# Moving q's product ahead of the transpositions in an attention loop, and reordering the loads and the constants of its opening

## The chip, the cores and the metric

The kernel runs on one core of a Trainium2 chip. The metric is the device time of one execution in microseconds (us); the time of a kernel is the median of its runs. The engines are TensorE (PE; its weight loads are listed as PEld), VectorE (DVE), ScalarE (ACT), GpSimd (POOL) and SyncE (SP), which here only issues DMAs. Each engine runs its instructions in the order of its own program and waits on semaphores for the others.

## What is computed

x is 8 x 256 x 128 (B batches, N rows, C columns). Attention has 16 heads of 64 with one key and value shared by all heads, a learned null key and value (the two rows of `cond_64`), a relative position bias that a small MLP produces, and a causal mask. A feed-forward part with simulated int8 quantisation follows.

```python
xn = ln(x, g_norm)
q = (xn @ Wq).reshape(b, n, 16, 64).transpose(0, 2, 1, 3)
kv = xn @ Wkv                              # k, v: one head
k, v = concat([null_k, k]), concat([null_v, v])
q = l2norm(q) * q_scale;  k = l2norm(k) * k_scale
sim = einsum('bhid,bjd->bhij', q, k) * 8 + bias   # bias from the MLP
attn = softmax(where(causal | ~mask, neg, sim))
y = ln(einsum('bhij,bjd->bhid', attn, v).reshape(b, n, 1024) @ Wout, g_out)
out = x + ffn_int8(y)                      # scales are maxima over all of y
```

## The kernel before

Everything stays on the core. The work of attention is cut into 32 groups: a batch b has four groups g = 0 to 3 of four heads each. `over_groups` (L103) runs a function `group(s)` for the first 30 of them on each engine; `Group` (L59) says which pieces of other batches and groups ride along. The last two groups, `ending`, are written out.

In group s, TensorE (L1010) makes: the values (L887, probabilities times v, into `val_ps`) of the group two before, `s.summed`; the scores of s in two pairs of heads (L865, banks `front` and `back`); the output products of `s.summed` (L843); the transpositions of the probabilities of the group before, `s.turned` (L931), two heads in the front banks, then the transposition of a quarter of q (L754), then two heads in the back banks; and at the end q's product (L740) for the quarter `s.made`, three passes in the fp32r form that together stand for fp32. Small products of the next batch's k, v and x ride in the transpositions (`low_make`, L909). A quarter of q is 128 rows times 8 heads.

A quarter of q then passes all engines: TensorE's product into the one bank `q_ps`; ScalarE squares it (`q_square`, L532) as the first thing of the next group; VectorE sums the squares per head (`q_norm2`, L1143), also first; GpSimd raises to the power -0.5 (`q_power`, L411) ahead of its probabilities; VectorE scales (`q_normalise`, L1147) between the two score pairs; TensorE transposes; VectorE copies (`qT_evac`, L1154). ScalarE's group (L611) is: square of q, exponentials of two heads of the group before, of two heads of s, then the four copies `pT_evac` (L593) that the values wait for. VectorE's group (L1323) is: q sums, copy of the values' bank (`oT_copy`, L1262), scores of the first pair (L1270), reciprocals, k and q scaling, scores of the second pair, reciprocals, `qT_evac`, and the statistics of x, k and y. GpSimd (L451) does the powers of k, y, x and q, then multiplies probabilities by the reciprocal row sums (`normalise`, L443), four instructions for a pair of heads.

The order on every engine is written out by hand. The opening prepares batch 0: SP (L337 to 348) loads x, the k/v weights, the q weights, the mask, the second layer's constants `b1b` and `g1b`, and more; ACT's queue (L495 to 502) loads the first layer's constants, w1, the key constants `condk`, `qs`, `ks` (semaphore `ld_keys`) and the null value. The MLP runs beside the first k, v and q: TensorE L776 to 807, VectorE L1175 to 1260, ScalarE L549 to 581, GpSimd L384 to 441. Its result, `table`, goes to DRAM and comes back as the bias of all rows (SP, L351 to 359). `q_ps0` (L267) names the four banks of the first batch's quarters; they are made by `q_make_first` (L749) in fp32, two passes each. `keep_busy` (L771) issues transpositions of the identity whose result nobody reads. `mask_min` (L1191) decides between the two variants of TensorE's program; `value_load` (L794) reads it.

## Time and profile before

| | |
|---|---|
| median of 3 runs | 299.69 us (299.69 to 299.98) |
| the profiled execution | 299.08 us |
| its span, first to last instruction | 297.3 us |
| granted clock of TensorE, mean | 0.970 |
| busy: PE, DVE, ACT, POOL | 257.9, 238.1, 230.0, 204.6 us |
| opening, up to the first scores of TensorE | 26.9 us |
| groups 0 to 3 | to about 60.8 us |
| six batches alike | 60.8 to 232.9 us |
| last groups, feed-forward part | to 297.3 us |

The profile is of one execution. Its times are in microseconds from the start of the span. A timeline row has the start, the duration, the engine, the line, the operation, what it writes and reads, and, in brackets, how long the engine stood idle before it and what released it. Rows with x3 or x8 are several instructions merged: the duration runs from the start of the first to the end of the last. Matmuls are pipelined, so the distance between two starts says more of TensorE than a duration. The granted clock (PEclk) is a share of 2.4 GHz.

### The profile page before, as it was taken

How to read it: one execution, taken by the hardware profiler on the slowest of the kernel's cores; microseconds unless marked ns; L12 is line 12 of the kernel's file. 1: busy time of each engine (PE TensorE's matmuls, PEld its weight loads, DVE VectorE, ACT ScalarE, POOL GpSimd, SP SyncE). 2: the span in 40 equal slices, each digit the busy share in tenths (PEclk: the TensorE clock that was granted, in tenths of full speed). 3: DMA queues.
4: the chain of work that ended last, by engine and by line, in shares of the span. 5: the costliest groups of instructions: out<-in, count | busy, mean ns of one | idle time of the engine just before them, and what ended most of it. 6: DMA issues, size and time to landing. Idle time of an engine off the chain costs nothing.

```text
span 297.3 us, 7308 instructions
## 1 busy us (share of the span) xinstructions
PE 257.9 (87%) x2161; PEld 203.5 (68%) x2162; DVE 238.1 (80%) x969; ACT 230.0 (77%) x781; POOL 204.6 (69%) x394
## 2 busy tenths in 40 slices
PE   0769999999999999999999999999999989975270
PEld 0427777787888778877887888788878767751060
DVE  2768978798879878888888798787877788869893
ACT  1554978888898899889988988889888897259380
POOL 2277979788878887887888888788877785013300
PEclk9989999999999999999999999999999999999857
DMA  4179100000000000000000000000000020000013
GB/s 142 33 191 264 21 1 2 1 2 1 3 0 2 4 1 2 0 3 1 2 0 4 3 0 2 0 4 0 2 0 4 1 73 3 2 0 0 1 37 110
DMA packets 13084, 6.89 MB, mean 23 GB/s; under 512 B 1954, under 2 KB 12914, under 8 KB 13043
## 3 DMA queue, kind: packets, MB, share of 16 engines
q1 hardware_dynamic: 11874, 6.03, 7.7%
q10 hardware_dynamic: 1168, 0.36, 0.6%
q8 instruction: 20, 0.33, 0.5%
q14 instruction: 22, 0.17, 0.2%
HBM read 5.31 MB, written 1.07 MB: 21 GB/s over the span
## 4 chain that ended last, share of the span: by engine, by line
PE 60%; DVE 20%; POOL 8%; issue 5%; DMA 4%; ACT 2%; SPq 1%; POOLq 0%; DVEq 0%; ACTq 0%
PE bank L904 14%; PE front L881 7%; PE bank L855 7%; PE back L947 7%; PE bank L744 6%; POOL prob L448 6%; PE back L881 5%; PE front L947 4%; DVE score L1276 4%; DMA g1b<-in_L_cond_g_dram 4%; PE bank L760 3%; DVE oT L1266 2%; DVE hmax L1428 2%; DVE oT L1464 2%; DVE yn L1299 1%
## 5 line engine op out<-in xcount | busy, mean ns | idle before, releaser
L589 ACT ACTIVATE prob<-score,negmax 128x258 f32<-128x258 f32 (+1 forms) x256 | 113.4, 449 | 17.8 <-DVE negmax L1276 17.7
L448 POOL TENSOR_SCALAR prob<-prob,rrow 128x258 f32<-128x258 f32 x254 | 107.9, 443 | 22.0 <-DVE rrow L1284 20.1
L401 POOL TENSOR_TENSOR rq<-qn,neghalf 128x8 f32<-128x8 f32 x32 | 53.3, 1666 | 2.7
L589 ACT ACTIVATION_READ_ACCUMULATOR prob<-score,negmax 128x1 f32 x256 | 49.2, 192 | 0.0
L904 PE MATMUL bank<-pT,val 128*64 128x256 f32 x496 | 47.1, 332 | 0.0
L1276 DVE CUSTOM_DVE_ANT_0 score<-front,bias 128x258 f32<-128x258 f32 (+1 forms) x128 | 38.2, 354 | 8.0 <-PE front L881 7.8
L904 PEld LDWEIGHTS bank<-pT,val 128*64 128x64 f32 x496 | 30.8, 136 | 19.3 <-ACT pT L599 9.9
L1145 DVE TENSOR_REDUCE qn<-sq 128x8 f32<-128x512 f32 x32 | 21.9, 684 | 23.7 <-ACT sq L535 23.7
L1276 DVE CUSTOM_DVE_ANT_0 score<-back,bias 128x258 f32<-128x258 f32 (+1 forms) x128 | 38.0, 353 | 0.1
L855 PE MATMUL bank<-wout,oT 128*128 128x128 f32 x256 | 36.7, 287 | 1.2 <-DVE yn L1299 1.1
L599 ACT COPY pT<-back 128x384 f32<-128x384 f32 x62 | 28.8, 481 | 9.0 <-PE back L947 8.6
L855 PEld LDWEIGHTS bank<-wout,oT 128*128 128x128 f32 x256 | 31.0, 191 | 5.5 <-DVE oT L1266 1.5
L947 PE MATMUL back<-ident,prob 128*128 128x128 f32 x192 | 30.4, 277 | 2.9 <-POOL prob L448 2.1
L881 PE MATMUL front<-kT,qT 64*128 64x258 f32 (+1 forms) x256 | 29.7, 350 | 0.3 <-DVE qT L1156 0.2
L947 PE MATMUL front<-ident,prob 128*128 128x128 f32 x192 | 29.6, 273 | 0.0
L599 ACT COPY pT<-front 128x384 f32<-128x384 f32 x62 | 26.9, 470 | 3.2 <-PE front L947 3.1
L881 PEld LDWEIGHTS front<-kT,qT 64*128 64x128 f32 x256 | 22.2, 186 | 7.5 <-issue 5.9
L881 PE MATMUL back<-kT,qT 64*128 64x258 f32 (+1 forms) x256 | 26.7, 327 | 0.0
L947 PEld LDWEIGHTS back<-ident,prob 128*128 128x128 f32 x192 | 21.2, 141 | 7.0 <-DVE negmax L1276 5.2
L1266 DVE COPY oT<-bank 128x512 f32<-128x512 f32 x32 | 22.1, 689 | 4.8 <-PE bank L904 2.2
L881 PEld LDWEIGHTS back<-kT,qT 64*128 64x128 f32 x256 | 22.3, 187 | 1.8 <-issue 0.3
L947 PEld LDWEIGHTS front<-ident,prob 128*128 128x128 f32 x192 | 22.8, 141 | 0.2 <-DVE negmax L1276 0.2
(203 smaller groups left out, 465.0 us busy)
## 6 DMA issues: line engine op xcount, KB each, us to landing
bias<-relative_table SPq DMA_DIRECT2D x8, 256.0 KB, 5.0
out_dram<-prob SPq DMA_DIRECT2D x4, 256.0 KB, 3.0
X<-in_x_dram SPq DMA_DIRECT2D x1, 896.0 KB, 13.9
prob<-in_L_cond_Wq_dram SPq DMA_DIRECT2D x1, 512.0 KB, 5.4
wout<-in_L_cond_Wout_dram SPq DMA_DIRECT2D x1, 512.0 KB, 15.1
prob<-in_L_ffn_w_down_dram SPq DMA_DIRECT2D x1, 176.0 KB, 2.4
X<-in_x_dram SPq DMA_DIRECT2D x1, 128.0 KB, 4.3
prob<-in_L_ffn_w_gate_dram SPq DMA_DIRECT2D x1, 128.0 KB, 2.2
```

Of the source, the lines that this page charges most:

```text
L401: pool.tensor_tensor(dst, src, neghalf[:, 0:width], ALU.pow).then_inc(done, 1)
L448: pool.tensor_scalar(prob[:, par, h, cols], prob[:, par, h, cols], rrow[:, par, h, t:t + 1], 1.0, ALU.mult, ALU.mult).then_inc(normed, 1)
L589: act.activation(prob[:, par, h, cols], score[:, h % 4, cols], ACT.Exp, scale=-1.0, bias=negmax[:, par, h, t:t + 1], accum_out=rowsum[:, p ...
L599: act.copy(pT[:, h % 4, :], bank[i][:, 0:3 * P]).then_inc(pT_ready, 1)
L744: last = pe.matmul(ps[:, :], xx[par][:, P * (q % 2):P * (q % 2) + P], ww[:, 512 * (q // 2):512 * (q // 2) + 512], start=xx is xTh and ww i ...
L855: pe.matmul(y_out(t), oT[:, m % 2, k, t * P:t * P + P], wout[:, k, :], start=k + t == 0, stop=False, skip_group_check=True)
L881: product = pe.matmul(banks[a][:, at:at + KEYS1 - c0], qT[par][rows, h // 2, t * P:t * P + P], kT[par][rows, c0:KEYS1], start=not masked, ...
L904: last = pe.matmul(ps[a * D:a * D + D, pair * N + i0:pair * N + N], val[m % 2][:, blk, :], turned[:, 2 * pair + a, c0:c1], start=blk == 1, ...
L947: product = pe.transpose(bank[i][:, k * P:k * P + P], prob[:, par, h, c0:c0 + P], ident[:, :])
L1145: dve.tensor_reduce(qn2[:, q, :], sq[:, :, :], AX.X, ALU.add).then_inc(q_n2, 1)
L1266: dve.tensor_copy(oT[:, m % 2, 2 * g:2 * g + 2, :].rearrange("p k n -> p (k n)"), (q_ps if at == GB * B - 1 else val_ps)[:, :])\
L1276: dve.tensor_tensor_reduce(score[:, h % 4, c0:c0 + w], ps[:, c0:c0 + w], bias[:, h, 0:w], -1.0, -3.0 * NEG, ALU.add, ALU.min, negmax[:, pa ...
```

## The change

Loads: `b1b` and `g1b` go ahead of the q weights and the mask on SP. GpSimd's four memsets of constants go ahead of its first power. In the opening ScalarE's mask row goes to the end, the second silu behind the squares of q's quarters 0 and 1; TensorE makes three quarters of q at once, and `keep_busy` calls are added. VectorE's `mask_min` and `table` go back in its order, and q's third scaling goes into group 0. In the loop q's product goes ahead of the transpositions, its square ahead of the pT copies, its sum ahead of `qT_evac`, its power behind the back heads' probabilities, and its scaling to the start of the next group. The values wait for their copies pair by pair. y's power goes from group 2 to group 1. The diff, cut to its core:

```diff
-        q_ps0 = [bank[i] for i in (5, 2, 3, 4)]
+        q_ps0 = [bank[i] for i in (5, 2, 4, 5)]
@@ sync
+            for dst, src in ((b1b[:, :], row(b1)), (g1b[:, :], row(g1))):
+                sp.dma_start(dst, src).then_inc(ld_mlp, 16)
             sp.dma_start(wq[:, :], Wq).then_inc(ld_wq, 16)
             sp.dma_start(mask_u[:, :], mask.rearrange("(a b) n -> a (b n)", a=1)).then_inc(ld_mask, 16)
-            for dst, src in ((b1b[:, :], row(b1)), (g1b[:, :], row(g1))):
-                sp.dma_start(dst, src).then_inc(ld_mlp, 16)
@@ gpsimd
             pool.memset(table[:, 0:P - 1], NEG).then_inc(table_pad, 1)
+            pool.memset(mrow[:, :, 0:KEYS1 + 1:P + 1], 0.0).then_inc(consts, 1)
+            pool.memset(vnull[:, :, :], 0.0).then_inc(consts, 1)
+            pool.memset(unull[:, :, :], 0.0).then_inc(null_zero, 1)
+            pool.memset(pnT[:, :], 0.0).then_inc(null_zero, 1)
...
             mlp_power(0)
-            pool.memset(mrow[:, :, 0:KEYS1 + 1:P + 1], 0.0).then_inc(consts, 1)
-            pool.memset(vnull[:, :, :], 0.0).then_inc(consts, 1)
-            pool.memset(unull[:, :, :], 0.0).then_inc(null_zero, 1)
-            pool.memset(pnT[:, :], 0.0).then_inc(null_zero, 1)
             mlp_power(1)
@@
             def group(s):
-                if s.kT is not None:
-                    k_power(s.kT)
-                if s.g == 2 and s.prev is not None:
-                    y_power(s.prev)
-                if s.g == 3 and s.b + 3 < B:
-                    x_power(s.b + 3)
-                if s.quarter is not None and s.quarter >= 4:
-                    q_power(s.quarter, s.quarter % 4)
                 if s.turned is not None:
                     normalise(heads(s.turned)[2:4])
                 if s.at == 2:
                     x_power(2)
+                if s.g == 3 and s.b + 3 < B:
+                    x_power(s.b + 3)
+                if s.g == 1 and s.prev is not None:
+                    y_power(s.prev)
+                if s.made is not None:
+                    q_power(s.made, s.made % 4)
+                if s.kv is not None:
+                    k_power(s.kv)
                 normalise(heads(s.at)[0:2])
@@ ending of gpsimd
-                y_power(B - 2)
@@ scalar, opening
             mlp_turned(0)
+            kv_evac(0, halves(misc))
+            q_square(0, q_ps0[0])
+            q_square(1, q_ps0[1])
+            mlp_silu(1)
+            mlp_turned(1)
+            q_square(2, q_ps0[2])
+            act.wait_ge(kT_done, 1)
+            for par in range(2):
+                act.copy(kT[par][:, 0:KEYS1:P + 1], misc[:, 2 * P:2 * P + 2]).then_inc(null_a, 1)
+            kT_evac(0, halves(misc))
+            v_copy(0)
+            act.activation(table_load[:, 1:2], neghalf[:, 0:1], ACT.Exp)
+            q_square(3, q_ps0[3])
+            act.wait_ge(wq_ready, 1)
+            act.copy(wqh[:, :], wq[:, :]).then_inc(wq_high, 1)
             act.wait_ge(ld_mask, 16)
...
             act.activation(keys1, mask_v, ACT.Copy, scale=-NEG, bias=NEG).then_inc(mask_ready, 1)
-            kv_evac(0, halves(misc))
-            q_square(0, q_ps0[0])
-            mlp_silu(1)
-            mlp_turned(1)
-            q_square(1, q_ps0[1])
-            act.activation(table_load[:, 1:2], neghalf[:, 0:1], ACT.Exp)
...
-            kT_evac(0, halves(misc))
-            v_copy(0)
-            for q in range(2):
-                q_square(q + 2, q_ps0[q + 2])
-            act.wait_ge(wq_ready, 1)
-            act.copy(wqh[:, :], wq[:, :]).then_inc(wq_high, 1)
@@ scalar, loop
             def group(s):
-                if s.quarter is not None and s.quarter >= 4:
-                    q_square(s.quarter, q_ps)
                 if s.turned is not None:
                     exponent(heads(s.turned)[2])
                     exponent(heads(s.turned)[3])
...
                 exponent(heads(s.at)[1])
+                if s.made is not None:
+                    q_square(s.made, q_ps)
                 if s.turned is not None:
                     pT_evac(s.turned, 0)
@@ tensor, opening
             def q_make_first(q):
+                if q == 3:
+                    pe.wait_ge(q_norm, 1)
...
                 last.then_inc(mlp_t, 1)
+                keep_busy(3, qT_ps)
                 pe.wait_ge(mlp_a, 2 * layer + 2)
...
             pe.wait_ge(consts, 3)
+            keep_busy(40, qT_ps)
             for t in range(2):
                 xT_make(0, t, halves(misc))
...
             q_make_first(1)
+            q_make_first(2)
             mlp_turn(1)
...
-            pe.wait_ge(min_ready, 1)
-            least = pe.value_load(mask_min[:, :])
...
-            q_make_first(2)
+            keep_busy(6, qT_ps)
             qT_make(0)
             q_make_first(3)
             pe.wait_ge(null_a, 2)
             pe.wait_ge(kT_ready, 1)
+            keep_busy(6, misc)
+            pe.wait_ge(min_ready, 1)
+            least = pe.value_load(mask_min[:, :])
             keep_busy(6, misc)
@@ tensor, scores
                 if s.at == 0 and pair == 1:
-                    pe.wait_ge(q_norm, 3)
+                    pe.wait_ge(q_norm, 2)
@@ tensor, values
-                if at == LOOP:
-                    pe.wait_ge(pTe_ready, GH)
-                else:
-                    pe.wait_ge(pT_ready, GH * (at if at > LOOP else at + 1))
...
                 for pair in range(2):
+                    if at == LOOP:
+                        pe.wait_ge(pTe_ready, 2 * pair + 2)
+                    else:
+                        pe.wait_ge(pT_ready, GH * (at - 1 if at > LOOP else at) + 2 * pair + 2)
@@ tensor, loop
                 if s.g == 1 and s.prev is not None:
                     y_null(s.prev)
+                if s.made is not None:
+                    if s.made % 4 == 0:
+                        if s.first:
+                            pe.wait_ge(wq_low, 1)
+                        pe.wait_ge(xT_low, s.next)
+                    q_make(s.made, s.made % 4, s.made // 4 % 2, q_ps)
                 if s.turned is not None:
                     turn(s, 0)
                     turn(s, 1)
...
                     turn(s, 3)
-                if s.made is not None:
...
-                    q_make(s.made, s.made % 4, s.made // 4 % 2, q_ps)
@@ vector, opening
-            dve.tensor_reduce(mask_min[:, :], mask_u[:, :].bitcast(U16), AX.X, ALU.min).then_inc(min_ready, 1)
...
+            k_norm2(0)
             dve.wait_ge(ld_keys, 16 * 3)
             dve.tensor_tensor_reduce(ksq[:, 2, :], condk[:, :], condk[:, :], 1.0, 0.0, ALU.mult, ALU.add,
                                      kn2[:, 2:3]).then_inc(null_v, 1)
-            k_norm2(0)
...
             q_norm2(0, 0)
-            dve.wait_ge(mlp_t, 4)
-            dve.wait_ge(ld_w2, 16 * 2)
-            dve.tensor_scalar(table[:, P - 1:TABW], bank[1][0:H, 0:N], b2c[:, 0:1], None, ALU.add).then_inc(mlp_v, 1)
+            q_norm2(1, 1)
             dve.wait_ge(qks_ready, 1)
             dve.wait_ge(k_rk, 1)
             k_scale_out(condk[:, :], 2)
             k_normalise(0)
-            q_norm2(1, 1)
+            dve.wait_ge(mlp_t, 4)
+            dve.wait_ge(ld_w2, 16 * 2)
+            dve.tensor_scalar(table[:, P - 1:TABW], bank[1][0:H, 0:N], b2c[:, 0:1], None, ALU.add).then_inc(mlp_v, 1)
             q_normalise(0, 0, q_ps0[0])
+            dve.tensor_reduce(mask_min[:, :], mask_u[:, :].bitcast(U16), AX.X, ALU.min).then_inc(min_ready, 1)
...
             q_norm2(3, 3)
-            q_normalise(2, 2, q_ps0[2])
             x_normalise(1)
@@ vector, loop
             def group(s):
-                if s.quarter >= 4:
-                    q_norm2(s.quarter, s.quarter % 4)
-                if s.summed is not None:
-                    oT_copy(s.summed)
                 if s.g == 2 and s.prev is not None:
                     y_normalise(s.prev)
+                    oT_copy(s.summed)
+                if s.quarter >= 4:
+                    q_normalise(s.quarter, s.quarter % 4, q_ps)
+                if s.summed is not None and not (s.g == 2 and s.prev is not None):
+                    oT_copy(s.summed)
+                if s.at == 1:
+                    xT_split_low(1, 1)
...
-                if s.quarter >= 4:
-                    q_normalise(s.quarter, s.quarter % 4, q_ps)
+                if s.at == 0:
+                    q_normalise(2, 2, q_ps0[2])
                 score_pair(heads(s.at)[2:4])
...
                 invert(heads(s.at)[0:2])
+                if s.g == 1 and s.prev is not None:
+                    y_stats(s.prev)
+                if s.made is not None:
+                    q_norm2(s.made, s.made % 4)
                 if s.quarter > 2:
                     qT_evac(s.quarter, s.quarter % 4, s.quarter // 4 % 2)
                 if s.at == 1:
-                    xT_split_low(1, 1)
                     x_stats(2)
```

In `ending` VectorE's `y_normalise(B - 2)` goes ahead of `oT_copy(LOOP - 2)`.

## Rows read from the trace of the kernel before

**Rows 1.** Busy us (x instructions) by engine in one batch, granted clock, DMA share, GB/s.
```profile
118.16:146.85 28.69, 28.28 (x253) 23.23 (x255) 24.54 (x109) 25.31 (x91) 24.01 (x48) 1.00 0.01 2
```
**Rows 2.** Waits from 60.77 to 232.95: us in total, times, longest us.
```profile
PEld back L947 <- DVE negmax L1276: 4.9, 12, 0.5
```
**Rows 3.** Timeline of TensorE in one group (start, duration).
```profile
154.09 1.52 PE L904 MATMUL bank<-pT,val 128*64 128x256 f32 x16
155.54 0.93 PE L881 MATMUL front<-kT,qT 64*128 64x258 f32 x8
...
159.41 0.51 PE L947 MATMUL back<-ident,prob 128*128 128x128 f32 x3
...
160.49 0.48 PE L744 MATMUL bank<-wqh,xTh 128*128 128x512 f32 x1
...
161.36 0.87 PE L904 MATMUL bank<-pT,val 128*64 128x256 f32 x8
```
**Rows 4.** Timeline of ScalarE at the end of that group.
```profile
160.77 0.48 ACT L599 COPY pT<-back 128x384 f32<-128x384 f32 x1 [0.33 <-PE back L947]
...
161.67 0.63 ACT L535 ACTIVATE sq<-bank 128x512 f32<-128x512 f32 x1
```
**Rows 5.** Timeline of VectorE: sum of q's squares, oT copy, q's scaling.
```profile
133.63 0.69 DVE L1145 TENSOR_REDUCE qn<-sq 128x8 f32<-128x512 f32 x1 [0.67 <-ACT sq L535]
134.23 0.68 DVE L1266 COPY oT<-bank 128x512 f32<-128x512 f32 x1
...
136.55 0.69 DVE L1151 TENSOR_TENSOR qn<-bank,rq 128x512 f32<-128x512 f32 x1
```
**Rows 6.** Timeline of GpSimd: q's clamp and power, four scalings of probabilities.
```profile
134.52 0.25 POOL L399 TENSOR_SCALAR qn<-qn 128x8 f32<-128x8 f32 x1 [0.33 <-DVE qn L1145]
134.85 1.67 POOL L401 TENSOR_TENSOR rq<-qn,neghalf 128x8 f32<-128x8 f32 x1
136.72 1.66 POOL L448 TENSOR_SCALAR prob<-prob,rrow 128x258 f32<-128x258 f32 x4 [0.21 <-DVE rrow L1284]
```
**Rows 7.** Chain of work that ended last, in the opening: start, us, what.
```profile
3.43 10.45 DMA g1b<-in_L_cond_g_dram
```
**Rows 8.** Timeline of all engines in the opening.
```profile
3.88 0.45 ACTq L499 DMA_DIRECT2D ks<-in_L_cond_k_scale_dram  x1
...
9.02 0.66 PE L713 MATMUL bank<-ident,xn 128*128 128x128 f32 x2 [9.02 <-DVE xn L1117]
...
10.29 1.19 DVE L1191 TENSOR_REDUCE mask_min<-mask_u 1x1 int32<-1x1024 uint16 x1
...
12.79 1.92 PE L751 MATMUL bank<-prob 128*128 128x512 f32 x2
...
13.97 0.42 DVE L1202 TENSOR_TENSOR prob<-front,b1b 128x256 f32<-128x256 f32 x1 [1.70 <-DMA g1b<-in_L_cond_g_dram]
...
16.52 0.69 ACT L542 ACTIVATE prob<-prob,mrs 128x128 f32<-128x128 f32 x2 [1.18 <-POOL mrs L401]
...
20.87 1.92 PE L751 MATMUL back<-prob 128*128 128x512 f32 x2
```
**Rows 9.** Timeline of VectorE's first scores and three idle stretches of TensorE.
```profile
28.39 0.42 DVE L1276 CUSTOM_DVE_ANT_0 score<-front,bias 128x258 f32<-128x258 f32 x1
...
36.90 0.48 PE L744 MATMUL bank<-wqh,xTh 128*128 128x512 f32 x1 [0.54 <-issue]
...
42.74 0.30 PE L727 MATMUL front<-ident,kz 128*128 128x128 f32 x1 [0.64 <-DVE kz L1134]
...
50.95 0.66 PE L760 MATMUL bank<-ident,qn 128*128 128x128 f32 x4 [0.39 <-DVE qn L1151]
```
**Rows 10.** DMA issues: count, KB, us from issue to landing.
```profile
b1b<-in_L_cond_b_dram SPq DMA_DIRECT2D x1, 64.0 KB, 6.3
...
ks<-in_L_cond_k_scale_dram ACTq DMA_DIRECT2D x1, 32.0 KB, 11.4
```
**Rows 11.** Busy us by engine and granted clock from 22 to 23, columns as in rows 1.
```profile
22.00:23.00 1.00, 1.00 (x3) 0.42 (x2) 0.00 (x0) 0.18 (x1) 1.00 (x2) 0.50 0.56 144
```

More of the change, by code:

```diff
@@ L761, in qT_make, with keep_busy @@
                 last.then_inc(qT_done, 1)
+            def keep_busy(count, ps):
+                for _ in range(count):
+                    pe.transpose(ps[:, 0:P], ident[:, :], ident[:, :])
             def mlp_turn(layer):
@@ L1356, in group @@
                     x_normalise(s.b + 2)
-                if s.g == 1 and s.prev is not None:
-                    y_stats(s.prev)
                 if s.g == 2 and s.b > 1:
```

14 lines of the change are left out of this document (2 added, 12 removed).

## The prediction

> **What bounds the kernel now.** I read the busy time by stretch first, then the waits of the loop, then one group of the loop engine by engine, and last the opening. The loop's batches take 28.69 us each and are alike; in one, TensorE's matmuls are busy 28.28 us, VectorE 24.54, ScalarE 25.31 and GpSimd 24.01 [rows 1]. So TensorE's own queue sets the pace and the others have 3 to 5 us a batch to spare. Only TensorE's small stalls can be won in the loop, plus what the opening wastes.
>
> Where are these stalls? VectorE's long waits, those for ScalarE's square of q, are off the path, since TensorE stays busy through them. What counts in the view of waits are the rows of TensorE: the back transpositions wait for VectorE's scores, 12 times in six batches, 4.9 us [rows 2]. In the group that starts at 154.09 the six back transpositions start at 159.41 and the next product at 160.49: 1.08 us for what unstalled costs 6 x 0.11 = 0.66, so 0.42 idle [rows 3]. In two of a batch's four groups this happens (here 0.42; about 0.2 in the milder one, an estimate from 4.9/12 = 0.41 of weight-load wait, half of which overlaps running matmuls). The second place: three q passes take 160.49 to 161.36 = 0.87 [rows 3], though their columns need only about 0.24 each (0.72, and some 0.07 for the change of form: 0.79). The missing 0.08 is the wait for the last pT copy: it starts at 160.77 and takes 0.48 [rows 4], so it ends at 161.25 and the values start 0.11 later. Four of those are 0.33 a batch. Idle in a batch is thus 0.42 + 0.2 + 0.33 = 0.95 to 1.0 us; in six batches 6 us. More than that the loop can't give.
>
> **The loop, part by part.** No work is added or removed; q's product, its square, its reduction, its power and its scaling each move.
>
> TensorE: three q passes (0.79) go from behind the back transpositions to ahead of the front ones. Every transposition starts 0.79 later against scores and probabilities, so the 0.42 and 0.2 vanish: both were smaller. What is late next: between the last back transposition and the values stood q as a filler of 0.87. Now nothing does. The path is last transposition's issue end, 0.28 to the copy's start, 0.48 copy, 0.11 to TensorE: 0.87 [rows 3, 4]. The split wait covers most of it: the first pair of values (half of 154.09 to 155.54, 0.73) [rows 3] needs only two copies. The remainder is 0.87 - 0.73 = 0.14 a group, 0.56 a batch, in place of 0.33. Net: 0.62 + 0.33 - 0.56 = 0.4 a batch, 2.4 us in six batches. Bounds: if queueing behind another copy adds 0.07, 0.28 a batch less, so 0.7 in all; if the remainder is hidden, 5.7.
>
> ScalarE: the square (0.63, [rows 4]) moves ahead of the four pT copies. It waits for q, which now ends some 5.1 us into a group, about when I step the exponentials to end (4.8), so it costs the copies 0.6; they are needed only from 6.9 on for the first pair. Hidden by 0.2.
>
> VectorE and GpSimd form the new risk. Now VectorE scales q by rq before its oT copy, and rq comes from GpSimd. The chain from one group to the next: y products 1.0, q 0.79, 0.2 to ScalarE, square 0.6, 0.07, reduction 0.69 [rows 5], 0.1, GpSimd's clamp and power 2.0 (134.52 to 134.85 + 1.67) [rows 6], 0.07, scaling 0.69 (0.62 until the next starts) and oT copy 0.68 [rows 5], 0.1 to the next y products: 6.8 to 6.9 us. A group takes 28.69/4 = 7.17 now and would take 7.07. So VectorE's waiting instruction holds oT copy and scores behind it, but ends some 0.2 us before TensorE asks. This is the narrowest cover of the change. Where GpSimd is busy when the reduction is done (the four probabilities, 1.66 [rows 6], start only when VectorE has inverted; a power of x or y, 0.97 at most, comes first), the chain gets longer by that overlap. I work out about 0.25 us of overlap in groups with a power of x; it eats 0.2 us, no more, and I leave it inside the bound.
>
> GpSimd otherwise gains: the probabilities of the back heads no longer stand behind a q power of 2.0 us.
>
> **The first groups.** Three idle stretches of TensorE stand here: 0.54 before the product of group 1, 0.64 before the turned k of group 2, 0.39 before q's transposition in group 3 [rows 9]. The first goes, since the low part of x is split earlier and q is asked for when VectorE is past it; the second is filled by the 0.79 of q, now ahead of it; the third came from rq standing behind two powers, and rq is now made half a group earlier. Sum 1.57, less 4 x 0.02: 1.5 us. Bounds 0.5 (only one of them) and 2.2.
>
> **The opening.** The chain now runs through g1b's landing: issued at 3.43, 10.45 us [rows 7], and VectorE's add waits 1.70 for it until 13.97 [rows 8]. Moved ahead of the q weights it should land near 8. Then the add waits for the product with w1, which I put at 11.6 to 12.4: the 1.19 us minimum of the mask [rows 8] is gone from ahead of it, but the q weights land later by b1b and g1b (0.35 + 0.45 of issue at least), and VectorE's scaling of them with it. That frees 1.6 us. But two things take it back. VectorE waits for the three key constants; ks lands 11.4 us after its issue at 3.88, at 15.3 [rows 8, 10]. And ScalarE's order has the second q square ahead of the second silu; that square waits for VectorE's first reduction, which is behind ks: 15.3 + 0.35 + 0.65 = 16.3. So silu 2 starts at 16.3 + 0.55 = 16.9 where it is 16.52 now [rows 8]. The table for the bias is then 0.3 us later, not earlier, and costs nothing as long as its loads land before the first scores (I expect 25.4 against 25.8).
>
> What gains is behind it. k's scaling follows at 17.6; three quarters of q are ready; TensorE is at full clock. From rows: the first q pieces took 0.86 a pass at 12.79 (two passes in bank 5, 1.92 with the drain), and the pieces made at 20.87 ran likewise, with a granted clock of 0.50 (1.2 GHz) in 22 to 23 [rows 8, 11]. The added transpositions (40, then 3, 3, 6, 6) use idle time; 40 cost 0.22 each at 1.2 GHz and 0.11 at 2.4, so from 1.5 us they end between 7.8 and 10.4. x is turned at 9.02 now [rows 8], so their bound is 0 to 1.4 us late; I take 0, since the clock rises on the way. The mask's minimum, 1.19, now stands between q's first scaling and the rest on VectorE, the path: it is paid there. ScalarE's mask row and the w_q split (some 3 us) end about 0.5 us before the first exponential. Stepping VectorE's queue: q scaled 20.2, minimum 21.4, reduction 22.0, qT 22.6, scaling 23.2, x statistics 23.9, qT 24.6, reduction 25.2, xn 25.8. The first scores, at 28.39 now [rows 9], come at 25.85; q's third scaling, moved into group 0, gives back 0.4. Gain 2.2 us; bounds 0 (silu, the power and ks all late) and 4.
>
> One rule speaks against the load order. Of g1b the row says that b1b, issued 0.39 us before it, landed after 6.3 us and g1b after 10.4 [rows 10]: landing is far from the order of issue. The Trainium skill, page "DMA: Bandwidth & Descriptors", section "Queues, rings and completion order", says that each engine takes turns between its queue rows and that completion isn't first in, first out; the trace agrees. By it g1b could still land near 13.9. As a mechanism of this kernel: ScalarE's queue has its own eight loads under way in that stretch. The add then stays at 13.97, the first reduction comes at 17.0 and silu 2 at 17.6: 0.7 us less than my sum, inside the bound.
>
> **Sum.** 2.4 + 1.5 + 2.2 = 6.1 us. The profiled execution took 299.08 (span 297.3 and 1.8 around it): 293.0. The median of the runs is 299.69, 0.6 above it: 293.6.
>
> **The rivals.**
> Loop gives nothing: the 0.14 at the values is 0.24, or the chain of 6.9 takes what was won. Sum 1.5 + 2.2: 296.0. For it: the cover is 0.2 us. Against: 3 to 5 us of slack an engine. 0.13.
> Opening gives nothing: ks and the ScalarE order hold all of it: 295.8. 0.08.
> It gives all: opening 4, first groups 2, loop 4.5: 289.2. 0.12.
> Neither does what it says, the waits only change place: 299.7, 0.05.
> **Slower:** the chain through GpSimd becomes the bound. Its place is VectorE's scaling of q ahead of oT copy; it decides from the point where the power begins over 0.3 us later than I have it (6.85 + 0.3 is a group of now). At 0.6 late a group is 7.45, 0.28 more, x 24 = 6.7 us; less 3.7 of the opening and first groups, about 302 to 303. For it: a 1.66 us block and a power of 0.97 share that queue. Against: VectorE inverts at 3.7 us into a group, the block ends at 5.6, the reduction at 6.3. 0.12.
>
> **How the numbers follow.** The forecast has 0.50, its own range 291.5 to 296. Range for 8 in 10: from 289.0 to 298.5, which leaves out the slower case 0.12, the case of no change 0.05 and the tail of the best one 0.03. Faster by over 0.2% (under 299.1; about what a measurement of this kernel can tell) is 0.50 + 0.13 + 0.08 + 0.12 = 0.83; same 0.05; slower 0.12.
>
> **What would show it.** Batches of 28.3 us; no wait of back transpositions on scores; a wait of 0.1 to 0.2 us in the middle of the values on ScalarE's copy; VectorE's wait for the square smaller and a new one for GpSimd's rq; first scores near 25.9; g1b landing under 9. I am wrong if oT copies end later than 3.1 us into a group, if y products wait for them, or if x is turned after 9.6.

## The result, and the profile after

The changed kernel takes 301.75 us (median; 300.96 to 303.23) where the kernel before takes 299.69: a ratio of 1.0083, 95% interval 1.0047 to 1.0119. It is slower, by 0.8%; 293.6 us, 6.1 less than before, was forecast. The profiled execution took 303.23 us, with a span of 301.4 and a mean granted clock of 0.969.

**Where the 4.1 us of span came from**, profiled execution against profiled execution. Up to VectorE's first scores: 28.63 against 28.39 [rows 9], +0.24. From there to the start of the values of group 4: 31.90 against 32.31, -0.41. Six batches, from the values of group 4 to those of group 28: 175.72 against 172.18, +3.54. The rest +0.73. So nearly all of it is in the loop, where 2.4 us of gain were forecast. (The first two are of one execution each: five kernels with after's opening, unchanged, have their first scores at 27.38 to 28.76, three with the old one at 27.97 to 28.39. A difference of a few tenths there says nothing.)

A batch of after, in the columns of [rows 1]:

```profile
119.62:149.14 29.52, 28.18 (x254) 23.48 (x255) 24.44 (x109) 24.78 (x92) 23.70 (x47) 1.00 0.01 2
```

TensorE is busy 28.18 us, 0.1 less than before, but the batch takes 29.52 where it took 28.69. By this view its idle time has grown from 0.41 to 1.34 us a batch. No engine is busy over 96% of the batch: the bound is no engine's work any more. It is a ring of waits: a chain of instructions on several engines that comes back to where it began, so that each turn can start only when the last one is through. The chain of the work that ended last says it too, by engine (before: PE 60%, DVE 20%, POOL 8%):

```profile
DVE 29%; PE 26%; POOL 18%; issue 12%; ACT 8%; DMA 4%; SPq 1%; POOLq 0%; DVEq 0%; ACTq 0%
```

Waits from 60 to 235 in after (us in total, times, longest):

```profile
DVE qn L1157 <- POOL rq L405: 24.2, 24, 1.9
ACT prob L588 <- DVE negmax L1281: 23.9, 24, 1.4
...
PEld bank L860 <- DVE oT L1271: 7.6, 12, 0.9
PE bank L860 <- DVE oT L1271: 5.2, 11, 0.7
...
PEld back L952 <- issue: 3.0, 6, 0.5
PE back L952 <- POOL prob L448: 1.8, 6, 0.3
...
ACT sq L534 <- PE bank L743: 1.5, 6, 0.3
...
PEld back L952 <- DVE negmax L1281: 0.3, 1, 0.3
```

The last row carries the name of what the change was to remove: 12 waits of the back transpositions, 4.9 us, put down to scores [rows 2]. One is left under that name. But six more, one a batch, are still there under "issue", 0.5 each, and TensorE's own row says what they wait for, before and after: GpSimd's probabilities.

```profile
160.21 0.52 PE L947 MATMUL back<-ident,prob 128*128 128x128 f32 x3 [0.29 <-POOL prob L448]
```

```profile
133.61 0.52 PE L952 MATMUL back<-ident,prob 128*128 128x128 f32 x3 [0.29 <-POOL prob L448]
```

The first rows are what came new. In each of 24 groups VectorE's scaling of q waits for GpSimd's power, 1.0 us on average. In three groups of four (all but g = 2, where it goes ahead) the oT copy that TensorE's output products (L860) need stands behind it in VectorE's queue, and in all four the next scores do. One group in detail, all from after. VectorE:

```profile
136.69 0.68 DVE L1271 COPY oT<-bank 128x512 f32<-128x512 f32 x1
137.29 0.41 DVE L1281 CUSTOM_DVE_ANT_0 score<-front,bias 128x258 f32<-128x258 f32 x1
...
140.13 0.69 DVE L1151 TENSOR_REDUCE qn<-sq 128x8 f32<-128x512 f32 x1 [0.30 <-ACT sq L534]
...
143.63 0.69 DVE L1157 TENSOR_TENSOR qn<-bank,rq 128x512 f32<-128x512 f32 x1 [1.89 <-POOL rq L405]
144.24 0.68 DVE L1271 COPY oT<-bank 128x512 f32<-128x512 f32 x1
144.84 0.42 DVE L1281 CUSTOM_DVE_ANT_0 score<-front,bias 128x258 f32<-128x258 f32 x1
```

ScalarE, first of the exponentials and the square of q that stands behind them:

```profile
137.75 0.51 ACT L588 ACTIVATE prob<-score,negmax 128x258 f32<-128x258 f32 x1 [0.80 <-DVE negmax L1281]
...
139.52 0.58 ACT L534 ACTIVATE sq<-bank 128x512 f32<-128x512 f32 x1
```

GpSimd:

```profile
138.78 1.66 POOL L448 TENSOR_SCALAR prob<-prob,rrow 128x258 f32<-128x258 f32 x4 [0.97 <-DVE rrow L1289]
140.52 0.19 POOL L401 TENSOR_SCALAR mv<-mv 128x2 f32<-128x2 f32 x1
140.79 0.71 POOL L405 TENSOR_TENSOR rstd<-mv,neghalf 128x2 f32<-128x2 f32 x1
141.59 0.25 POOL L403 TENSOR_SCALAR qn<-qn 128x8 f32<-128x8 f32 x1
141.93 1.67 POOL L405 TENSOR_TENSOR rq<-qn,neghalf 128x8 f32<-128x8 f32 x1
```

TensorE at both ends of the group:

```profile
137.42 1.16 PE L860 MATMUL bank<-wout,oT 128*128 128x128 f32 x8 [0.33 <-DVE oT L1271]
...
144.97 1.16 PE L860 MATMUL bank<-wout,oT 128*128 128x128 f32 x8 [0.72 <-DVE oT L1271]
```

This is a ring: scores (137.29), exponentials (137.75), square (139.52), sum (140.13), clamp and power on GpSimd (141.59 to 143.60), scaling (143.63), oT copy (144.24), and again scores (144.84). One turn takes 7.55 us here, more than the 7.17 of a group before. The first scores on VectorE start at 122.28, 130.33, 137.29 and 144.84, and those of the next group at 151.79. So the four turns of a batch are 8.05, 6.96, 7.55 and 6.95, together 29.51: the whole batch, but for rounding. Where nothing stands in its way the ring takes 6.96. The power of x (140.52 to 141.50) adds 0.59. In group 1 the statistics of y stand ahead of q's sum on VectorE, and the power of y ahead of q's on GpSimd:

```profile
125.57 0.46 DVE L1295 BATCH_NORM_STATS2 ost<-bank 128x6 f32<-128x128 f32 x2
126.17 0.25 DVE L1298 BATCH_NORM_AGGREGATE omv<-ost 128x2 f32<-128x6 f32 x2
126.34 0.65 DVE L1151 TENSOR_REDUCE qn<-sq 128x8 f32<-128x512 f32 x1
```

The square was done at 125.47 there, its sum starts at 126.34, and the turn is 1.09 longer than the plain one. From the rows of the two turns: the square starts 0.36 later after the scores (it waits for q's product, which TensorE makes behind the products of the null value), its sum another 0.86 (the statistics of y), the power 0.47 (y's power ahead of it); and 0.60 comes off again, as the oT copy goes ahead of q's scaling in group 2.

**The opening after.** The load of the q weights, issued behind `b1b` and `g1b`, landed 10.5 us after its issue; before, it was issued at 2.19 and landed after 5.4. The chain of work of after has it where [rows 7] has g1b:

```profile
3.13 10.53 DMA prob<-in_L_cond_Wq_dram
```

VectorE's scaling of these weights stands ahead of everything that follows from the MLP:

```profile
13.69 0.75 DVE L1195 TENSOR_SCALAR prob<-prob,gcol 128x1024 f32<-128x1024 f32 x1 [4.64 <-DMA prob<-in_L_cond_Wq_dram]
...
15.14 0.40 DVE L1207 TENSOR_TENSOR prob<-front,b1b 128x256 f32<-128x256 f32 x1
...
21.46 0.47 DVE L1224 TENSOR_SCALAR table<-front,b2c 16x256 f32<-16x256 f32 x1 [1.10 <-PE front L796]
22.46 1.20 DVE L1227 TENSOR_REDUCE mask_min<-mask_u 1x1 int32<-1x1024 uint16 x1
28.63 0.43 DVE L1281 CUSTOM_DVE_ANT_0 score<-front,bias 128x258 f32<-128x258 f32 x1 [0.22 <-PE front L886]
```

The add of the MLP (L1207) no longer waits for g1b, and is at 15.14 where it was at 13.97 [rows 8]. On ScalarE the second square of q stands ahead of the second silu, and waits 2.01 us:

```profile
18.26 0.60 ACT L534 ACTIVATE sq<-back 128x512 f32<-128x512 f32 x1 [2.01 <-DVE qn L1151]
18.75 0.68 ACT L541 ACTIVATE prob<-prob,mrs 128x128 f32<-128x128 f32 x2
```

### The profile page after: what moved, and what is told of

It reads as the page before. It is cut to its first block, busy times and chain, and to the rows that moved or that the text cites. A ratio compares the mean times of both kernels' runs of the same rounds, so it can differ in the third digit from the quotient of the medians.

```text
span 301.4 us, 7424 instructions
## 1 busy us (share of the span) xinstructions
PE 262.2 (87%) x2220; PEld 212.2 (70%) x2220; DVE 236.7 (79%) x969; ACT 226.2 (75%) x781; POOL 202.7 (67%) x394
## 4 chain that ended last, share of the span: by engine, by line
DVE 29%; PE 26%; POOL 18%; issue 12%; ACT 8%; DMA 4%; SPq 1%; POOLq 0%; DVEq 0%; ACTq 0%
POOL rq L405 11%; DVE score L1281 7%; PE bank L909 5%; ACT prob L588 5%; POOL prob L448 4%; DMA prob<-in_L_cond_Wq_dram 3%; PE bank L860 3%; PE front L886 3%; DVE oT L1271 2%; PE back L886 2%; DVE qn L1151 2%; PE bank L743 2%; PE back L952 2%; DVE hmax L1437 2%; PE front L952 2%
## 5 line engine op out<-in xcount | busy, mean ns | idle before, releaser
L448 POOL TENSOR_SCALAR prob<-prob,rrow 128x258 f32<-128x258 f32 x254 | 105.7, 436 | 24.9 <-DVE rrow L1289 21.9
L1157 DVE TENSOR_TENSOR qn<-bank,rq 128x512 f32<-128x512 f32 x31 | 21.4, 691 | 29.0 <-POOL rq L405 29.0
L860 PE MATMUL bank<-wout,oT 128*128 128x128 f32 x256 | 36.9, 288 | 8.0 <-DVE oT L1271 7.9
L860 PEld LDWEIGHTS bank<-wout,oT 128*128 128x128 f32 x256 | 31.0, 191 | 13.1 <-DVE oT L1271 11.3
L952 PE MATMUL back<-ident,prob 128*128 128x128 f32 x192 | 28.6, 275 | 2.4 <-POOL prob L448 2.2
L598 ACT COPY pT<-back 128x384 f32<-128x384 f32 x62 | 27.3, 481 | 4.5 <-PE back L952 3.3
## 6 DMA issues: line engine op xcount, KB each, us to landing
prob<-in_L_cond_Wq_dram SPq DMA_DIRECT2D x1, 512.0 KB, 10.5
```

The costliest lines, as they stand in the source:

```text
L448: pool.tensor_scalar(prob[:, par, h, cols], prob[:, par, h, cols], rrow[:, par, h, t:t + 1], 1.0, ALU.mult, ALU.mult).then_inc(normed, 1)
L598: act.copy(pT[:, h % 4, :], bank[i][:, 0:3 * P]).then_inc(pT_ready, 1)
L860: pe.matmul(y_out(t), oT[:, m % 2, k, t * P:t * P + P], wout[:, k, :], start=k + t == 0, stop=False, skip_group_check=True)
L952: product = pe.transpose(bank[i][:, k * P:k * P + P], prob[:, par, h, c0:c0 + P], ident[:, :])
L1157: dve.tensor_tensor(qn[:, :, :], ps[:, :].rearrange("p (h d) -> p h d", d=D), rq[:, q, :].unsqueeze(2).broadcast_to([P, 8, D]), ALU.mult). ...
```

## The experiments

The ratios are to the kernel before on the same chip, whose median was 298.19 to 298.85 us, with 95% intervals.

**Two halves.** One kernel has after's opening and before's loop, the other before's opening and after's loop.

> The changed opening (loads, banks, three quarters of q ahead, the 40 transpositions) with the loop of the kernel before. Theory: the whole loss is in the loop, where VectorE, ScalarE and GpSimd form a ring (scores, exponentials, square of q, its sum, its power, its scaling, oT copy, next scores) that is now longer than TensorE's work; then batches are 28.7 us again, the first scores come near 28.6 as in the changed kernel and the time is within 0.5 us of the kernel before, 299.2 to 300.2. Rival, the opening costs the 2 us (the q weights landed at 13.7 there): 301 to 302 with batches of 28.7.

Measured: 298.68 us, ratio 1.0013 [0.9991, 1.0035]; batches of 28.67 to 28.70 us.

> The opening of the kernel before with the changed loop (product, square, sum, power and scaling of q moved, values waiting pair by pair). Theory of the ring: batches of 29.5 us as in the changed kernel, time 301 to 302.5. Rival, the opening costs: batches at or below 28.7 and 299.7 or less.

Measured: 301.22 us, ratio 1.0088 [1.0058, 1.0118]; batches of 29.46. The loop holds the loss, and the opening moves nothing that can be measured.

**The ring, cut at VectorE.** In the changed kernel the oT copy always goes ahead of the scaling of q.

```diff
                 if s.g == 2 and s.prev is not None:
                     y_normalise(s.prev)
+                if s.summed is not None:
                     oT_copy(s.summed)
                 if s.quarter >= 4:
                     q_normalise(s.quarter, s.quarter % 4, q_ps)
-                if s.summed is not None and not (s.g == 2 and s.prev is not None):
-                    oT_copy(s.summed)
```

> The changed kernel, VectorE's oT copy always ahead of q's scaling. Theory of the ring: 0.60 us (the oT copy) leaves it in the groups g = 0, 1 and 3 of a batch, where the steps were 6.96, 6.96 and 7.55 us; the fourth, 8.05, had it so already. The ring's sum falls from 29.5 to 27.7 a batch, under TensorE's work of some 28.1, so TensorE's queue sets the pace again: batches of 28.1 to 28.6, time 294.5 to 297. Rival, it is the place of q's product on TensorE (the transpositions come later and the values wait for the last copy) that costs: no change, 301 to 302.5.

Measured: 294.43 us, ratio 0.9857 [0.9825, 0.9889]. One batch, and the waits from 60 to 232:

```profile
116.20:144.25 28.05, 27.95 (x253) 23.52 (x255) 24.20 (x109) 24.66 (x92) 23.73 (x47) 1.00 0.01 2
```

```profile
DVE oT L1271 <- PE bank L909: 15.7, 20, 1.4
...
DVE qn L1157 <- POOL rq L405: 3.2, 6, 0.7
```

TensorE is busy 27.95 of 28.05 us. The wait for GpSimd's power falls from 24.2 to 3.2 us, and VectorE now waits for TensorE's values, as it should where TensorE is the bound. The edit takes 6.7 us off the time (by the two ratios, 1.0083 and 0.9857) and nothing from the work, so the ring through the oT copy is shown to be the cause, not only argued. It also shows what the changed loop is worth without the ring: a batch is 0.64 us shorter than before.

**The ring, shortened at GpSimd.** Two kernels from the changed one, with VectorE's order left as it is. In the first q's power goes ahead of those of x and y:

```diff
+                if s.made is not None:
+                    q_power(s.made, s.made % 4)
                 if s.g == 3 and s.b + 3 < B:
                     x_power(s.b + 3)
                 if s.g == 1 and s.prev is not None:
                     y_power(s.prev)
-                if s.made is not None:
-                    q_power(s.made, s.made % 4)
```

> The changed kernel, GpSimd's power of q ahead of the powers of x and y (a clamp and a power each, 0.97 us with the gaps). Theory of the ring: the step of 7.55 (the power of x stands between the probabilities and q's power) falls to 6.96 and that of 8.05 (the power of y) by about 0.5; a batch 29.5 - 1.1 = 28.4, time 295 to 297. Rival, TensorE's order: no change, 301 to 302.5.

Measured: 311.32 us, ratio 1.0432 [1.0402, 1.0462], the other way by far. Its waits from 60 to 240:

```profile
ACT prob L588 <- DVE negmax L1281: 29.0, 21, 3.0
POOL qn L403 <- DVE qn L1151: 20.6, 23, 1.7
POOL prob L448 <- DVE rrow L1289: 17.6, 13, 1.6
DVE yn L1304 <- POOL ors L405: 16.1, 6, 2.7
```

The last row is the reason: in group 2 VectorE's first instruction is y's normalisation, which needs y's power, and all of VectorE's group stands behind it: 2.7 us, six times. I had costed y's power as free to move. The second kernel leaves it ahead and moves only x's power (of group 3) behind q's.

> The changed kernel with GpSimd's power of q ahead of the power of x (group g = 3) alone; the power of y stays where it is. With both moved the kernel was 9.6 us slower than the changed one, since VectorE scales y at the very start of group 2 and waited up to 2.7 us for a power of y that now stood behind q's. Theory of the ring: without that, the step of group 3 falls from 7.55 to about 6.96 us, a batch to 28.9, and the time to 298 to 299. Rival, the power order on GpSimd costs in itself: 301 to 302 or more.

Measured: 300.29 us, ratio 1.0058 [1.0033, 1.0084], over the 298 to 299 that I expected; the interval spans much of that of the changed kernel, so the time alone doesn't tell the two apart. The batch does: 29.16, 0.36 shorter. The place is right: the turn with x's power takes 7.22 (scores at 106.16 and 113.38) where it took 7.55. The 0.26 that are missing from 0.59 stand in one row of GpSimd, beside one of VectorE:

```profile
110.20 1.93 POOL L405 TENSOR_TENSOR rq<-qn,neghalf 128x8 f32<-128x8 f32 x1
```

```profile
110.20 0.41 DVE L1128 TENSOR_TENSOR xTl<-xTr,xTh 128x256 fp32r<-128x256 f32 x1
```

q's power takes 1.93 instead of 1.67, because it now starts together with an addition of VectorE (below).

**The values' wait, alone.** In the kernel before, only the wait of the values is split into pairs, and nothing else.

```diff
-                if at == LOOP:
-                    pe.wait_ge(pTe_ready, GH)
-                else:
-                    pe.wait_ge(pT_ready, GH * (at if at > LOOP else at + 1))
...
+                    if at == LOOP:
+                        pe.wait_ge(pTe_ready, 2 * pair + 2)
+                    else:
+                        pe.wait_ge(pT_ready, GH * (at - 1 if at > LOOP else at) + 2 * pair + 2)
```

> The kernel before with one edit: the values wait for their pT copies pair by pair. I put the wait of the values behind q's passes at 0.08 us a group; all of it should go, since the first pair needs copies that are long done and takes 0.73 us. Expected 0.33 us less in each of six batches and as much in the first groups, 28.36 a batch, 2.0 to 2.4 us less than the kernel before. Rival, the 0.08 us is the change of form between products and no wait: no change.

Measured: 298.05 us, ratio 0.998 [0.9952, 1.0008], and a batch of 28.68. The 0.08 us ahead of the values, which I had read as a wait for the last copy, is not one: with the wait made earlier it stays.

**The opening, in the kernel with the oT copy first.** In one kernel the loads go back to the old order (`Wq` and the mask ahead of `b1b` and `g1b`), in another the 40 transpositions are left out, in a third both.

> oT copy first, and the loads in the order of the kernel before (q weights and mask ahead of b1b and g1b). Theory: the q weights, which landed 10.5 us after their issue in the changed kernel against 5.4 before, land near 7.6 again and VectorE scales them at 9 instead of 13.7; b1b's sum is then held by g1b at 13.9 instead of 15.1. First scores at 27.0 to 27.6 against 28.66 with oT copy first alone; time 293.0 to 293.8 against 294.43. Rival, the bias loads or the key constants set the first scores: no change, 294.2 to 294.7.

Measured: 293.84 us, ratio 0.9828 [0.9795, 0.9861]. First scores at 28.43, not 27.0 to 27.6. The weights of q are scaled at 9.37 instead of 13.69, but then VectorE's add waits for g1b, as before the change:

```profile
13.85 0.42 DVE L1207 TENSOR_TENSOR prob<-front,b1b 128x256 f32<-128x256 f32 x1 [2.96 <-DMA g1b<-in_L_cond_g_dram]
```

One of the two loads is late in either order. The first scores are 0.23 earlier, within the scatter of this opening, and the interval overlaps that of oT_first. The rest of what I expected went together with a fall of TensorE's clock. TensorE had no work from 14.8 on; columns as in [rows 1]:

```profile
17.00:18.00 1.00, 0.00 (x0) 0.00 (x0) 0.37 (x1) 1.00 (x3) 0.92 (x3) 0.55 1.22 290
18.00:19.00 1.00, 0.77 (x4) 0.78 (x5) 1.00 (x4) 0.22 (x2) 1.00 (x1) 0.50 1.11 264
```

> oT copy first without the 40 transpositions of the identity at the start. They bring TensorE to full clock before x is turned at 8.9; the second product then ran at 1.0 us for four passes' issue instead of 1.0 for two. Theory of the opening: the products hang on the late q weights and the key constants, so 0.0 to 0.6 us is lost without them: 294.4 to 295.0. Rival, the full clock is what holds the opening together: 1.5 us or more lost, 296 and up.

Measured: 293.39 us, ratio 0.982 [0.9793, 0.9848]. First scores at 26.80 where the kernel with the 40 has 28.66, and a granted clock of 1.00 from 19 to 27, where that kernel has 0.50 from 21 to 24. I had expected a loss of up to 0.6 us; the ratio is 0.0037 lower, with intervals that overlap. The loads are in the new order here, so I tested the same with the old order:

> The kernel after with VectorE's oT copy first, the loads in their old order, and without the 40 transpositions of the identity. It differs from oT_loads in these 40 alone. In oT_loads TensorE ran out of work at 14.8, and its granted clock was 0.55 at 17 and 0.50 from 18 to 23; the first scores came at 28.43. Theory 1 (the clock falls because TensorE has no work from 14.8 to 18.2, whatever it did before): the clock falls here too, at 17 to 18, the table is made at 20.5, the first scores come at 28.4, and the time is that of oT_loads, a ratio to the kernel before of 0.981 to 0.985. Theory 2 (what TensorE did before 9 us counts: with the 40 the clock falls some 18 us after the start, without them it holds): the clock stays at 1.00, the table is made at 20.0, the first scores come at 26.6, ratio 0.976 to 0.980.

Measured: 292.36 us, ratio 0.9804 [0.9774, 0.9835]; first scores at 26.44, table at 19.69. By the trace theory 2 holds; the ratio lies between the ranges of the two theories, and settles nothing. TensorE is idle for 2.38 us here (3.42 in oT_loads), has no work from 17 to 18.14 either, and the clock stays:

```profile
17.00:18.00 1.00, 0.00 (x0) 0.00 (x0) 0.46 (x1) 1.00 (x3) 0.92 (x3) 1.00 1.22 290
18.00:19.00 1.00, 0.77 (x5) 0.53 (x5) 1.00 (x4) 0.47 (x3) 1.00 (x1) 1.00 1.04 247
```

**What the first scores wait for.** Two more edits: the second silu goes ahead of the second square of q on ScalarE (with VectorE's sum of that square behind the scaling of k), and the mask's minimum returns to its old place on VectorE, where that engine waits for g1b.

```diff
             q_square(0, q_ps0[0])
-            q_square(1, q_ps0[1])
             mlp_silu(1)
             mlp_turned(1)
+            q_square(1, q_ps0[1])
```

> oT_no40 with ScalarE's second silu ahead of its second square of q, and VectorE's second reduction of q behind the scaling of k. In oT_no40 the MLP's rsqrt is ready at 16.53, but silu 2 starts at 17.72 because the square ahead of it waited until 17.23 for VectorE's first reduction. Theory (the order on ScalarE holds back the bias table): silu 2 starts at 16.7, the table is made at 19.0 to 19.6 in place of 20.00, and the first scores come 0.4 to 1.0 earlier than 26.80, because they wait for the bias loads; ratio to the kernel before 0.978 to 0.981, where oT_no40 had 0.982. Rival (the bias isn't what the first scores wait for; the scaling and turning of q are): the table comes earlier, the first scores stay at 26.8 or come later by up to 0.5, since q's second reduction has lost its gap; ratio 0.982 to 0.984.

Measured: 292.59 us, ratio 0.9806 [0.9769, 0.9843]. Silu 2 starts at 17.00, but the table is at 20.52, later than 20.00. Three things are in that. The q weights landed 0.4 us later in this execution than in oT_no40. TensorE made the three quarters of q more slowly: their starts are 1.87 and 1.70 apart (13.84, 15.71, 17.41) where oT_no40 has 1.33 and 0.86, so that the MLP's second turning, behind them in its queue, started at 18.60, 0.9 after the silu was done (17.00 + 0.69), and nothing of the earlier silu was left. And the sum of the square, which I had put ahead of the table, now waits for ScalarE:

```profile
19.92 0.69 DVE L1150 TENSOR_REDUCE qn<-sq 128x8 f32<-128x512 f32 x1 [0.72 <-ACT sq L534]
20.52 0.46 DVE L1223 TENSOR_SCALAR table<-front,b2c 16x256 f32<-16x256 f32 x1
```

First scores at 27.27. That is on the rival's side, but the table was not earlier, so the run didn't put the question; and its interval spans that of oT_no40.

> no40_loads with the minimum of the mask back at its old place on VectorE, where that engine waits for g1b (2.96 us idle in oT_loads). It takes 1.20 us, between q's first scaling and its third reduction, out of VectorE's queue. Theory (the minimum stands on the path of q to the first scores, paid in full): first scores 1.0 to 1.2 earlier than in no40_loads, ratio lower by 0.003 to 0.004. Rival (the first scores wait for the bias loads, which are issued when the table has gone out to DRAM): 0 to 0.3 earlier, and a wait of VectorE for the bias before the first scores; ratio within 0.001 of no40_loads.

Measured: 292.14 us, ratio 0.9801 [0.9771, 0.983], against 0.9804 without the edit. The rival holds, by its wait: VectorE could begin the first scores at 26.14 (26.44 with the minimum in its way), but they wait for the bias and start at 26.59:

```profile
26.59 0.43 DVE L1280 CUSTOM_DVE_ANT_0 score<-front,bias 128x258 f32<-128x258 f32 x1 [0.45 <-DMA bias<-relative_table]
```

> no40_min and no40_silu together: old order of the loads, no 40 transpositions, the mask's minimum at its old place, the second silu ahead of the second square of q, oT copy first. With both the table and q early, neither can hide the other. Theory: silu 2 at 16.5, table at 19.3, bias loads landed by 25.8, first scores at 25.6 to 25.9, which is what the prediction had; ratio 0.973 to 0.977. Rival (the clock of TensorE falls again, or GpSimd's powers of q take the place: the second of them ends at 21.8 in oT_no40): first scores at 26.5 to 27, ratio 0.979 to 0.982.

Measured: 290.84 us, ratio 0.9751 [0.9721, 0.9781], the fastest of all: 7.3 us less than the kernel before beside it, and by the ratios 9.9 less than the change. Silu 2 at 16.07, and on VectorE:

```profile
18.80 0.46 DVE L1224 TENSOR_SCALAR table<-front,b2c 16x256 f32<-16x256 f32 x1
...
25.88 0.43 DVE L1280 CUSTOM_DVE_ANT_0 score<-front,bias 128x258 f32<-128x258 f32 x1 [0.74 <-DMA bias<-relative_table]
```

Its chain of work before the first scores:

```profile
19.29 1.50 DMA relative_table<-table
...
21.21 4.50 DMA bias<-relative_table
```

The first scores are where the prediction had them (25.85), but not by its path: the table goes to DRAM and back in 6.9 us (18.80 to 25.71), and that now comes last. Alone, the minimum gave 0.2 us (292.36 to 292.14); the silu's place on top of it gives 1.3 (290.84), together 1.5. That the bias covered part of the minimum's gain is shown by the wait of 0.45. Whether the silu's is covered by the minimum isn't shown: it was tried alone only with the loads in their new order, in the execution with the slow quarters of q. The intervals of no40_loads and no40_all overlap a little (0.9774 and 0.9781), and the profiled spans, one execution each (290.2 and 290.1), don't order them.

## Why the prediction was wrong

**What bounds the kernel: right, and the start of the error.** TensorE was the bound before [rows 1]. From "3 to 5 us a batch to spare" I concluded that the others could take on order. Busy time says nothing of that: after the change all four engines have less to do in a batch, and the batch is 0.83 longer.

**The back transpositions' wait: half right.** I took both stalls of a batch for waits on scores, and 0.42 + 0.2 as gone. The milder is gone. The one that I read, at 159.41, stays: its second half waited for GpSimd's probabilities at 160.21, not for scores, and after the change it is the row at 133.61. In the kernel with the oT copy first it is still there in four of six batches. **The values: wrong.** The 0.33 a batch "for the last pT copy" was never a wait, as split_only shows; the last q pass stands 0.33 ahead of the values there too (0.32 before). I put it down to the change of form, which I had sized from another row, but no run shows that. I read a coincidence (the copy ended 0.11 before) as a release, though the row carries no bracket. The 0.56 that I set against it did not come either: with the oT copy first, TensorE idles 0.10 us in a batch. Loop without the ring: 0.64 a batch, 3.8 in six, for 0.4 and 2.4 forecast (bounds 0.7 and 5.7). That this comes near is partly luck, as three of its terms were wrong, in both directions.

**The ring: this is the step that failed.** I worked out the turn as 6.8 to 6.9 us (my terms add up to 6.92); it is 6.96 where nothing is in the way. That size was right, its path only in part: I closed it through TensorE's output products and q's product. In the trace the exponentials of the scores reach the square last in three groups of four, 0.96, 0.24 and 0.23 after q's product; only in group 1 is the product last, by 0.26. What failed is the sentence "about 0.25 us of overlap in groups with a power of x; it eats 0.2 us, no more". I stepped a plain group and took the 0.2 us between 6.9 and 7.07 as cover for the others. But x's power stands just ahead of q's and takes 1.0: it costs 0.59. And I stepped no group with y, where q's product, the statistics of y and y's power all come in the way: 1.09 net. The sum to make was that of the ring over a batch, 4 x 6.96 + 0.59 + 1.09 = 29.52, against TensorE's 28.3. It is 1.2 us longer, so the loop lost 3.5 us in six batches where I had 2.4 of gain.

**The slower rival: right in place, near in time by luck.** "VectorE's scaling of q ahead of oT copy", at 0.6 late a group, 302 to 303: measured 301.75, and in that place. But it took 6.7 us of loss in the loop less 3.7 of gain ahead of it, and the runs have 3.5 of loss and 0.2 of gain: two errors of over 3 us that cancel. It had a chance of 0.12. The argument against it, "VectorE inverts at 3.7 us into a group, the block ends at 5.6, the reduction at 6.3", looked at one plain group. I had named this cover as the narrowest, and should have stepped all four groups of a batch, as there are only four.

**The first groups: right in size, hidden by the ring.** From the first scores to group 4's values: 32.31 before, 30.93 with the oT copy first, a gain of 1.38 for 1.5 forecast. By place it was less exact, so part of the agreement is luck: the first and third idle stretch go, the second [rows 9] stays at 0.53 of 0.64, and a new one of 0.33 stands at 37.98. In after, waits of 0.82 and 0.69 for the oT copy took 1.0 of it.

**The opening: the second step that failed, 0 in place of 2.2.** g1b did land earlier, at 10.75 (2.65 + 8.1; before 13.9), and the product with w1 was there at 11.7. But the q weights, which I put "0.35 + 0.45" later, landed 6.1 us later (at 13.66 for 7.6). Their scaling stands ahead of the add in VectorE's queue, and so the wait changed its name and place only: 4.64 us for `Wq` in place of 1.70 for g1b. The Trainium skill, page "DMA: Bandwidth & Descriptors", section "Queues, rings and completion order", says that completion isn't first in, first out, and I feared that for g1b. These three loads show none of it: they land in the order of issue, before (Wq 7.6, b1b 9.3, g1b 13.9) and after (b1b 6.6, g1b 10.8, Wq 13.7), and my "landing is far from the order of issue" misread the two rows of [rows 10]. What they show is that a place further back cost the large load 5.1 us more from issue to landing, where I had charged it the issue cost alone. **ScalarE's order: right.** Silu 2 comes behind the square's wait for the first sum, as I wrote; it is at 18.75, and not 16.9, because the add is at 15.14 and not near 12, and the first sum ends at 18.16 where I had 16.3. **"TensorE is at full clock": wrong for most of it.** The first three quarters of q, from 14.49 on, do run faster (starts 0.97 and 0.86 apart, where before had 1.71), but the granted clock is 0.50 from 20 to 23 in after, as it was from 21 to 23 before. **The minimum: half right.** It is on q's path, but the bias comes next: without the minimum the first scores wait 0.45 for it.

**The range** (289.0 to 298.5) left the slower case out, and by my own chances it could; 301.75 is that case, and what was wrong was its 0.12.

## What to carry to other kernels

Before a value that comes back from another engine is used ahead of an instruction that the bounding engine waits for, follow the ring through one whole period, every kind of group in it, add each instruction that stands ahead on each queue, and compare the sum with the bounding engine's work: the busy shares say nothing of it. Where a load is moved, ask for each load that it passes who waits for it in order. And where two waits cover each other, an experiment that removes one shows next to nothing: remove both.

## What was not expected of the hardware

**With work early on, TensorE's clock was lower later.** The 40 transpositions do raise the clock: in after the four products with w1 take 0.71 us at 10.97; without the 40 they take 1.22, as at half the clock, though the granted clock reads 1.00 in both. But all six kernels that have the 40 also show a stretch at 0.50 later in the opening. It begins at 17 while TensorE stood idle for 3.42 us (oT_loads), at 19 to 20.8 in four (in oT_first 1.5 us after an idle stretch of 2.15), and at 11 in pow_first, where the clock was back at 1.00 from 18 on and the first scores came at 27.38. Without the 40, with idle stretches of 1.78 (oT_no40) and 2.38 (no40_loads) at the same place, it stayed at 1.00, and so it did in the three kernels built on these. That is one profiled execution of each kernel. In time the effect is small and not clear of the noise: by their ratios, leaving out the 40 is worth 0.0037 (oT_no40 against oT_first) and 0.0024 (no40_loads against oT_loads), 0.7 to 1.1 us, and each pair's intervals overlap. The first scores come 1.9 us earlier in each of these pairs, but only 0.6 lies between oT_no40 (26.80) and pow_first. The kernel before, and two more with its opening, have no such transpositions either, and there the clock fell at 20 all the same (in before after idle stretches of 0.85, 0.46 and 1.44 us), so the early work isn't all that counts. What decides stays open.

**GpSimd's power beside VectorE.** In xpow_first the power of q takes 1.67 us in 19 of 24 groups and 1.93 or 1.94 in five, and these five are the ones that start with L1128, VectorE's addition of `xTr` and `xTh`. The Trainium skill, page "GPSIMD Engine Reference", section "1. Specifications", says that the two engines share interfaces to the memory, and contend where a VectorE instruction has two inputs from it; L1128 has two, and the trace agrees, at 0.26 us. In after, where the addition starts 0.6 us ahead of the power (141.33 and 141.93), the power takes 1.67.

**A load of 512 KB behind two small ones.** `Wq` landed 5.4 us after its issue when it was ahead of `b1b` and `g1b` (64 KB each), and 10.5 us when it was issued behind them, 0.94 us later, while the two landed after 4.4 and 8.1 instead of 6.3 and 10.4. It is so in all kernels here: `Wq` took 5.4 to 6.1 us in the seven with the old order and 9.5 to 10.5 in the seven with the new one.
